# Four channel mixes of a MetaFormer block: fp32 matmuls on two row tiles in place of products of fp16 high and low halves

## The reference

```python
x = x + conv(_ln_c(x), w_pc, w_in, fft_w, w_out)      # _ln_c: normalised over the 48 channels
t = tokens(x); t = t + ffn(_ln_t(t), W1, b1, W2, b2)   # operands in fp8 e5m2, sums rounded to fp16

def conv(x, w_pc, w_in, fft_w, w_out):
    x1 = conv3x3(x[:, :12], w_pc)                      # 12 of the 48 channels
    x = concatenate([x1, x[:, 12:]], axis=1)
    x = conv1x1(x, w_in)                               # 48 -> 254 channels: the "mix"
    xf = rfft2(patches_8x8(x)) * fft_w                 # one weight for each channel and frequency
    a, b = split(irfft2(xf), 2, axis=1)
    return conv1x1(gelu(a, approximate=False) * b, w_out)   # 127 -> 48 channels
```

## Time and profile before

| | |
|---|---|
| median of 3 runs | 703.85 us (702.35 to 704.34) |
| the profiled execution's own time | 702.13 us |
| its span, first to last instruction | 700.3 us |
| mean granted clock of TensorE | 0.988 |
| matmuls (PE) busy | 664.4 us, 95% |
| weight loads (PEld) busy | 522.9 us, 75% |
| VectorE (DVE) busy | 596.9 us, 85% |
| ScalarE (ACT) busy | 536.6 us, 77% |
| GpSimd (POOL) busy | 460.9 us, 66% |

### The profile page before, as it was taken

How to read it: one execution, slowest core, us unless ns; L and a number is a source line. 1 busy time by engine, 2 the same in 40 slices (tenths; PEclk the granted TensorE clock), 3 DMA queues, 4 the chain that set the end, 5 groups by cost and what they waited for, 6 DMA issues and landing times.

```text
span 700.3 us, 19259 instructions
## 1 busy us (share of the span) xinstructions
PE 664.4 (95%) x6713; PEld 522.9 (75%) x6713; DVE 596.9 (85%) x1151; ACT 536.6 (77%) x1080; POOL 460.9 (66%) x355
## 2 busy tenths in 40 slices
PE   1689999999999999999999999999999999999984
PEld 1577778877777788777877887778778877787751
DVE  5537888889898889898999888988988899877877
ACT  3144479888888898888888988888889888877784
POOL 2555656778667767786776677867676777653353
PEclk9999999999999999999999999999999999999995
DMA  3443333333434343344344432343444324331102
GB/s 83 87 104 89 86 73 102 99 79 90 106 91 109 94 105 94 81 92 103 93 109 94 107 102 74 89 106 91 101 102 105 100 59 109 78 85 46 47 22 69
DMA packets 47959, 62.23 MB, mean 89 GB/s; under 512 B 20607, under 2 KB 36439, under 8 KB 47863
## 3 DMA queue, kind: packets, MB, share of 16 engines
q1 hardware_dynamic: 45015, 60.52, 34.9%
q10 hardware_dynamic: 2848, 0.48, 0.4%
HBM read 44.62 MB, written 16.35 MB: 87 GB/s over the span
## 4 chain that ended last, share of the span: by engine, by line
PE 87%; DVE 6%; SPq 2%; issue 2%; POOL 1%; ACT 1%; DMA 0%; DVEq 0%; ACTq 0%; POOLq 0%
PE inva L483 16%; PE invb L490 16%; PE mixp L470 13%; PE misc L734 8%; PE misc L499 7%; PE misc L554 4%; PE misc L520 4%; PE misc L598 4%; PE misc L470 3%; PE misc L719 3%; PE misc L529 2%; PE mixp L567 2%; PE misc L588 2%; PE mixp L574 2%; DVE gmix L1144 1%
## 5 line engine op out<-in xcount | busy, mean ns | idle before, releaser
L483 PEld LDWEIGHTS inva<-inv,gmix 128*127 128x127 f32 x1024 | 126.2, 191 | 16.5 <-DVE gmix L1144 11.5
L483 PE MATMUL inva<-inv,gmix 128*127 128x128 f32 x1024 | 137.9, 277 | 0.6 <-DVE gmix L1144 0.6
L490 PE MATMUL invb<-inv,gmix 128*127 128x128 f32 x1024 | 134.7, 274 | 0.2
L1144 DVE TENSOR_TENSOR gmix<-mixp,freq_w 128x508 f32<-128x508 f32 x192 | 122.7, 681 | 14.0 <-PE mixp L470 13.5
L1452 POOL TENSOR_TENSOR st<-st,neg_half 128x16 f32<-128x16 f32 x32 | 92.8, 2899 | 60.6 <-DVE st L1366 60.6
L490 PEld LDWEIGHTS invb<-inv,gmix 128*127 128x127 f32 x1024 | 123.7, 191 | 1.4 <-DVE hbuf L1155 0.6
L816 ACT ACTIVATE hid<-misc 128x512 f16<-128x512 f32 x180 | 98.0, 601 | 17.6 <-PE misc L554 17.6
L1155 DVE TENSOR_TENSOR hbuf<-gact,invb 127x512 f32<-127x512 f32 x128 | 87.5, 684 | 24.3 <-ACT gact L808 18.7
L1483 POOL TENSOR_TENSOR st<-st,neg_half 128x16 f32<-128x16 f32 x31 | 95.4, 3077 | 16.4 <-DVE st L1223 16.4
L825 ACT ACTIVATE hid<-hid 128x512 fp8e5<-128x512 f16 x174 | 93.2, 618 | 0.0
L808 ACT ACTIVATE gact<-inva 127x512 f32<-127x512 f32 x128 | 76.9, 601 | 20.6 <-PE inva L483 20.0
(11 more groups left out here) (178 smaller groups left out, 1369.2 us busy)
## 6 DMA issues: line engine op xcount, KB each, us to landing
xin<-in_x_dram SPq DMA_DIRECT2D x64, 192.0 KB, 3.3
xres<-in_x_dram SPq DMA_DIRECT2D x64, 192.0 KB, 4.2
out_dram<-ob SPq DMA_DIRECT2D x60, 192.0 KB, 2.7
taps<-cz_scratch SPq DMA_DIRECT2D x32, 292.5 KB
crm<-rm_scratch SPq DMA_DIRECT2D x64, 96.0 KB
cz_scratch<-cz SPq DMA_DIRECT2D x64, 48.8 KB
cx<-in_x_dram SPq DMA_DIRECT2D x32, 96.0 KB
rm_scratch<-rm_t SPq DMA_DIRECT2D x120, 4.0 KB
```

The source lines that it names most:

```text
L483: mm = pe.matmul(inva[0:HID, q * PX:(q + 1) * PX], gmix[:, s % 2, q, 0:HID], inv[:], start=True, stop=True, skip_group_check=True)
L490: mm = pe.matmul(invb[0:HID, q * PX:(q + 1) * PX], gmix[:, s % 2, q, HID:HID2], inv[:], start=True, stop=True, skip_group_check=True)
L1144: dve.tensor_tensor(gmix[:, s % 2, 2 * q:2 * q + 2, 0:HID2], pair[q][:, 0:2 * HID2].rearrange("p (e c) -> p e c", e=2), freq_w[:], ALU.mul ...
```

## The change

The coefficients are copied once, in fp32, to `zc` (by the same ScalarE instruction), and `win` is one fp32 matrix on both row tiles. A mix is then four fp32 matmuls in place of 16 fp16 ones. The subtraction `low_parts` and its semaphore go, and what waited for `lo_ready` waits for `coef_ready`, which ScalarE's copy raises. At the end of the kernel `zh` also served as a buffer for the last result; a tile `y_last` of its own takes that place.

```diff
-        win32 = sb("win32", [KC, HID2])
-        win = sb("win", [128, 2, HID2], F16)
+        win = sb("win", [128, HID2])
...
-        zh = sb("zh", [128, PAIRS, 128], F16)
-        zl = sb("zl", [128, PAIRS, 128], F16)
+        zc = sb("zc", [128, PAIRS, 128])
+        y_last = sb("y_last", [SPAN, PAIRS, PX], F16)
...
                 for e in range(2):
-                    for zpart, wpart in ((zh, 0), (zl, 0), (zh, 1), (zl, 1)):
-                        for q in range(2):
-                            r0 = HALF * q
-                            mm = pe.matmul(pair[q][:, e * HID2:(e + 1) * HID2],
-                                           zpart[r0:r0 + KC, 2 * s + e, :], win[r0:r0 + KC, wpart, :],
-                                           start=(e == 0 and zpart is zh and wpart == 0),
-                                           stop=(zpart is zl and wpart == 1), skip_group_check=True)
-                            if e == 1 and zpart is zl and wpart == 1:
-                                mm.then_inc(mix_done, 1)
+                    for q in range(2):
+                        y0 = HALF * q
+                        mm = pe.matmul(pair[q][:, e * HID2:(e + 1) * HID2], zc[y0:y0 + KC, 2 * s + e, :],
+                                       win[y0:y0 + KC, :], start=(e == 0), stop=True, skip_group_check=True)
+                        if e == 1:
+                            mm.then_inc(mix_done, 1)
...
-                        act.activation(zh[0:KSPAN, 4 * q:4 * q + 4, :].rearrange("p i c -> p (i c)"),
-                                       bank[(3, 0)[q]][0:KSPAN, :], ACT.Copy).then_inc(hi_ready, 1)
+                        act.activation(zc[0:KSPAN, 4 * q:4 * q + 4, :].rearrange("p i c -> p (i c)"),
+                                       bank[(3, 0)[q]][0:KSPAN, :], ACT.Copy).then_inc(coef_ready, 1)
...
-                dve.tensor_scalar(win32[:], inva[0:KC, 0:HID2], SCALE, None, ALU.mult).then_inc(set_dve, 1)
+                for base in (0, HALF):
+                    dve.tensor_scalar(win[base:base + KC, :], inva[0:KC, 0:HID2], SCALE, None, ALU.mult)\
+                       .then_inc(set_dve, 1)
...
-                for base in (0, HALF):
-                    dve.tensor_copy(win[base:base + KC, 0, :], win32[:]).then_inc(set_dve, 1)
...
-                dve.tensor_tensor(win[0:KC, 1, :], win32[:], win[0:KC, 0, :], ALU.subtract).then_inc(set_dve, 1)
...
-                dve.tensor_copy(win[HALF:HALF + KC, 1, :], win[0:KC, 1, :]).then_inc(set_done, 1)
-                dve.wait_ge(set_done, 1)
+                dve.sem_inc(set_done, 1)
...
-            def low_parts(t, q):
-
-                n = at(t, 3)
-                dve.wait_ge(hi_ready, upto(2 * n + q + 1))
-                dve.tensor_tensor(zl[0:KSPAN, 4 * q:4 * q + 4, :].rearrange("p i c -> p (i c)"),
-                                  bank[(3, 0)[q]][0:KSPAN, :],
-                                  zh[0:KSPAN, 4 * q:4 * q + 4, :].rearrange("p i c -> p (i c)"),
-                                  ALU.subtract).then_inc(lo_ready, 1)
...
-                if live(t, 3):
-                    low_parts(t, 0)
-                    low_parts(t, 1)
```

More of the change, by code:

```diff
@@ L193, in metaformer_kernel @@
         conv_read = sem("conv_read")
-        hi_ready = sem("hi_ready")
+        coef_ready = sem("coef_ready")
         gelu_ready = sem("gelu_ready")
@@ L212, in metaformer_kernel @@
         mr_ready = sem("mr_ready")
-        lo_ready = sem("lo_ready")
         gmix_ready = sem("gmix_ready")
@@ L460, in mix @@
                     if s % 2 == 0:
-                        pe.wait_ge(lo_ready, s // 2 + 1)
+                        pe.wait_ge(coef_ready, s // 2 + 1)
                 elif s == 0:
-                    pe.wait_ge(lo_ready, upto(2 * n + 2))
+                    pe.wait_ge(coef_ready, upto(2 * n + 2))
                 pe.wait_ge(gmix_ready, upto(8 * n + 2 * (s if s != 1 else 0)))
@@ L639, in drain @@
                 t = (0, DRAIN)
-                pe.wait_ge(lo_ready, 2 * STEPS)
+                pe.wait_ge(coef_ready, 2 * STEPS)
                 pe.wait_ge(h_ready, 4 * NEW + 2)
@@ L704, in step @@
                     pe.wait_ge(conv_read, upto(before(2)))
-                    pe.wait_ge(lo_ready, upto(2 * before(3)))
+                    pe.wait_ge(coef_ready, upto(2 * before(3)))
                     pe.wait_ge(tsq_ready, upto(2 * before(4)))
@@ L744, in step @@
                     mix(t, 0)
-                    pe.wait_ge(lo_ready, upto(2 * n + 2, 2 * STEPS))
+                    pe.wait_ge(coef_ready, upto(2 * n + 2, 2 * STEPS))
                     pe.wait_ge(xsq_ready, upto(2 * a + 2, 2 * STEPS))
@@ L748, in step @@
                 if live(t, 4):
-                    pe.wait_ge(lo_ready, upto(2 * n + 1, 2 * STEPS))
+                    pe.wait_ge(coef_ready, upto(2 * n + 1, 2 * STEPS))
                     project(t, 0, bank[3])
@@ L976, in drain @@
                 sum_half(OLD, 1, inva, y16)
-                sum_half(NEW, 0, bank[2], zh)
+                sum_half(NEW, 0, bank[2], y_last)
                 convert(NEW, 1, 0)
-                sum_half(NEW, 1, invb, zh)
+                sum_half(NEW, 1, invb, y_last)
                 for half in range(2):
@@ L1092, in setup @@
                     dve.tensor_copy(freq_w[:, e, :], mixp[1][:, 0:HID2]).then_inc(set_dve, 1)
-                dve.wait_ge(set_dve, 12 + 14)
+                dve.wait_ge(set_dve, 12 + 15)
                 dve.tensor_copy(l1h[:], l1[:]).then_inc(set_dve, 1)
@@ L1096, in setup @@
                 dve.tensor_copy(eye8[:], eye[:], saturate=False).then_inc(set_dve, 1)
-                for base in (0, HALF):
-                    dve.tensor_copy(win[base:base + KC, 0, :], win32[:]).then_inc(set_dve, 1)
                 dve.tensor_copy(wpc[:, :, 0:CC], pc32[:]).then_inc(set_dve, 1)
+                dve.wait_ge(set_dve, 12 + 18)
+                dve.tensor_tensor(wpc[:, :, CC:2 * CC], pc32[:], wpc[:, :, 0:CC], ALU.subtract).then_inc(set_dve, 1)
                 dve.wait_ge(set_dve, 12 + 19)
-                dve.tensor_tensor(win[0:KC, 1, :], win32[:], win[0:KC, 0, :], ALU.subtract).then_inc(set_dve, 1)
-                dve.tensor_tensor(wpc[:, :, CC:2 * CC], pc32[:], wpc[:, :, 0:CC], ALU.subtract).then_inc(set_dve, 1)
-                dve.wait_ge(set_dve, 12 + 21)
-                dve.tensor_copy(win[HALF:HALF + KC, 1, :], win[0:KC, 1, :]).then_inc(set_done, 1)
-                dve.wait_ge(set_done, 1)
+                dve.sem_inc(set_done, 1)
                 second_channels()
@@ L1108, in setup @@
                 dve.tensor_copy(b8[:], raw_b[:], saturate=False).then_inc(set_dve, 1)
-                dve.wait_ge(set_dve, 12 + 22)
+                dve.wait_ge(set_dve, 12 + 20)
                 dve.tensor_copy(bq[:], b8[:]).then_inc(set_dve, 1)
-                dve.wait_ge(set_dve, 12 + 23)
+                dve.wait_ge(set_dve, 12 + 21)
             def second_channels():
@@ L1296, in output_half @@
                                       tch[0:SPAN, NEW % 4, 4 * c:4 * c + 4].rearrange("p i (r w) -> p i r w", w=TW),
-                                      zh[0:SPAN, 4 * c:4 * c + 4, :].rearrange("p i (r w) -> p i r w", w=TW),
+                                      y_last[0:SPAN, 4 * c:4 * c + 4, :].rearrange("p i (r w) -> p i r w", w=TW),
                                       ALU.add).then_inc(late_out, 1)
@@ L1328, in drain @@
                 bias_half(OLD, 1, y16)
-                bias_half(NEW, 0, zh)
+                bias_half(NEW, 0, y_last)
                 output_half(0)
-                bias_half(NEW, 1, zh)
+                bias_half(NEW, 1, y_last)
                 output_half(1)
```

## The result

The changed kernel took 709.43 us (median of 5 runs, 707.83 to 709.82) where the kernel before, timed beside it, took 704.34: ratio 1.0076, 95% interval 1.0054 to 1.0098. It is 0.8% slower. Its profiled execution took 707.83 us, 5.70 more than that of before, over a span 5.7 longer.

A forecast was written before the change was run, and what follows sets the result against it. The prediction took TensorE's own instruction stream as the bound. Streaming -1.3, entries +8.9 and prologue -0.7 us summed to +6.9 on 703.85, so 710.7 us; its own range was 705.7 to 714, for 8 in 10 702 to 725.

The forecast's parts named there:

- The forecast case: Whole kernel: 710.7 us, 1.0% slower; 706 to 714 us given a chance of 0.68.
- the prologue term: VectorE's work before the steps: three kinds of operation go, one copy comes, taken as -0.7 us, or 0 if L1119's data is late.
- What bounds the kernel: Steady steps: only TensorE's own instruction stream sets the time; 0.1 us in a step's stream is 3.2 us over 32 steps.
- The freed VectorE time: VectorE without the subtractions: some 42 us less busy, worth nothing, turning into idle time ahead of gate L1155.
- Streaming: TensorE's matmuls inside a mix: 0.860 us in fp32 against 0.870 in fp16, -1.3 us over 128 mixes.
- The entry: First matmul after a tiling change, mixes 0, 2 and 3: 102 ns excess instead of 9, +8.9 us over 96 entries.
- The choice of L483's row over L499's: Entry excess taken from an fp32 row of 127 columns, 102 ns, not one of 64 columns, 50 ns, giving +3.9 us.
- The step: One pipeline step: 20.17 us in place of 19.96, +0.21, with TensorE still busy throughout.
- Entry free: Rival for the first matmul after a tiling change: fp32 load hides like fp16's, 701.9 us, not slower; chance 0.10.
- Loads one after the other: Rival for the mixes: two row tiles load in turn, entry 204 ns, +20.3 us in all, 724 us; chance 0.09.
- Strict order: Rival for the mixes: records start strictly in order, one distance more a run, +20.6 us on top, 731 us; chance 0.07.
- No overlap: Rival for the mixes: fp32 row tiles don't run side by side, +110 us on top, 820 us; chance 0.06.

The follow-up runs named there:

- Experiments 3: Kernel before the change without VectorE's two subtractions a step, mixes using the high half twice: 702.31 us, ratio 0.9999.
- experiment 5: Changed kernel with VectorE's two subtractions put back in their original form, read from the banks, mixes waiting for them, result unused: 707.98 us, ratio 1.008.
- Experiment 1: Changed kernel with mix 3 moved behind two of the three first-layer matmuls that followed it, one fp32 entry less: 707.1 us, ratio 1.0066.
- experiment 6: Changed kernel, mixes 0 and 1 in 64-column pieces: 707.99 us; in 32-column pieces with mix 3 moved behind two first-layer matmuls: 706.09 us.
- experiment 7: Changed kernel with a mix's loops exchanged, both patch pairs of row tile 0 before both of tile 1: 711.52 us, ratio 1.0132.
- experiment 8: Kernel before the change without the product of the two low halves: 690.3 us; two variants also weighing mix 0 earlier on VectorE: 703.84 and 699.83 us.
- last variant of experiment 8: Kernel before the change with three products, mix 0 weighed ahead of the three short operations that end the statistics: 699.83 us, ratio 0.9955.
- experiment 4: Changed kernel plus two dummy VectorE subtractions a step, both operands from SBUF, result unused: 719.72 us, ratio 1.0242.

## Why the prediction was right

The forecast case came about: 709.43 us against 710.7, by the mechanism named, with 5.7 us measured (by spans) against 6.9 summed. That the sum is so near is in part luck: the prologue term was 0.7 us off one way, single longer steps 0.9 and the steps at both ends 1.0 the other way.

**What bounds the kernel.** Right. Experiments 3 and 5 take the subtractions away and put them back without moving a step; the stream alone counts in the usual step. The freed VectorE time turned up as idle time ahead of the gate, as said. What the prediction didn't see is how near VectorE was: the second layer's first weight load starts 0.115 us behind the end of mix 0's weighing, its first matmul at the earliest 0.146 behind it, and in the usual step of before that matmul comes 0.218 behind it. So 0.07 us were to spare there, and 0.14 in the changed kernel, whose longer mix 0 stands behind the start of that chain.

**Streaming.** 0.857 us for a mix measured, 0.860 estimated, in pairs. The interpolation from 128 and 512 columns held to 1 ns a slot.

**The entry.** 104 ns measured for 102 taken, 96 times, on both tiles' loads under one excess. Experiment 1 removes one and gets 0.095 us back, experiment 6 shows that it goes with the columns of the load. The choice of L483's row over L499's, by the columns, was the one that mattered. The Trainium skill, "TensorE: Matmul & The Clock Gate", section on weight-path perf modes, has the fast weight load for 128 non-fp32 weights alone, and the runs agree in kind. From its column rule the prediction worked out an estimate of 80 ns for the difference; here it is 104 - 9 = 95. That estimate took a quarter of the load's time for the fast load, which the section's table gives as theory for fp8; for fp16 weights the trace has loads of 93 ns against 187 in fp32, a half.

**The step.** 20.17 predicted and measured (+0.21 summed, +0.22 measured). 28 full steps at +0.22 are 6.15 us. The prediction took the difference for all 32.

**The prologue term failed.** -0.7 was taken, -0.04 came: the first operation on the channels starts at 28.00 instead of 28.04, the first forward transform at 41.69 instead of 41.73. VectorE's last operation ahead of the channel work ended at 27.37, near the 27.3 foreseen, and then this row:

```profile
27.18 0.19 DVE L1096 TENSOR_TENSOR wpc<-pc,wpc 72x36 f16<-72x36 f32 x1
28.00 0.42 DVE L1112 TENSOR_TENSOR cz<-cx,crm 96x256 f32<-96x256 f32 x1 [0.63 <-DMA crm<-rm_scratch]
```

The case was named (data not there earlier makes it 0) and the wrong side chosen: the trace of before showed no wait there, because VectorE itself was late, and I took that for data that was ready.

**What offset it.** The three steps that fill the pipeline grew by 0.16, 0.16 and 0.15 us, 0.47 in all: their entries grew like the others', but 0.06 to 0.08 us in each came off a wait of TensorE for another engine. The last step's mixes stand in the tail, which took 45.96 us in both. Single steps longer than the rest made up 1.46 us in the execution of before and 0.58 in that of after, -0.89. So 6.15 + 0.47 - 0.04 - 0.89 = 5.69 of the 5.7. The prediction had no term for such steps, and took the 0.7 us of waits for all there was. By distances between starts it was 1.2 us in four steps: the list counts only from where the matmul before is modelled to have ended. In all four, and in the three of the changed kernel, the second layer's first matmul starts 0.146 us behind the end of the weighing, so VectorE was what was late. A fifth step of before is 0.17 us longer ahead of mix 0, where the trace names VectorE's subtraction once. Whether the change alters the number of such steps is not shown, since each kernel has one trace: without the subtractions experiment 1 had 1.8 us of them, with them experiment 5 had 0.7.

**The rivals.** *Entry free*: out, by the 478 ns. *Loads one after the other*: out, one excess of 104 ns for two tiles, and distances of 0.214. *Strict order*: out by the pairs, and by experiment 7, where even four records of one tile in a row don't hold back the other. The Trainium skill's sentence on the same page, that matmuls start strictly in program order, doesn't fit two tiles with records of different tiles queued like this; the measurement decides. *No overlap*: out.

## What to carry to other kernels

When TensorE's stream is full, count in distances between starts, and give each run of same-tiled matmuls an entry cost of its own: here 0.1 us more for an fp32 load of 128 columns, on top of a streaming cost that was level. Work removed from an engine that waits for TensorE brings nothing, and its measure is an experiment that puts it back in exactly the same form (operands in the same memory). On VectorE beside a busy GpSimd, moving an operation by one microsecond can cost more than the wait it was moved for: look at what each operation will then stand beside. And a list of waits that is nearly empty says little of the slack behind it: measure how long ahead of its use each result is ready (here 0.07 us).

## What the runs showed of the hardware that was not expected

**VectorE operations held by GpSimd.** In the kernel before this happens in every step where it costs nothing: L1217, 16 elements, takes 0.80 us and ends 0.03 behind GpSimd's L1479, and L1204, 1024 elements in fp16, takes 1.44 where it takes 0.48 in the last variant of experiment 8. Rarely it costs something: L1359, 16 elements, usually 0.17 us, takes 0.63, and ends 0.02 to 0.03 us behind GpSimd's L1420. VectorE, GpSimd, the weighing and the weight load behind it, and what TensorE's second layer then waits:

```profile
201.52 0.63 DVE L1359 SCALAR_TENSOR_TENSOR st<-st 128x16 f32<-128x16 f32 x1
...
201.47 0.66 POOL L1420 TENSOR_TENSOR cz<-cz 96x256 f16<-96x256 f32 x1
...
203.08 0.68 DVE L1144 TENSOR_TENSOR gmix<-mixp,freq_w 128x508 f32<-128x508 f32 x1
203.88 0.17 PEld L567 LDWEIGHTS mixp<-hid,l 128*64 128x64 fp8e5 x4 [1.08 <-issue]
203.91 0.62 PE L567 MATMUL mixp<-hid,l 128*64 128x512 fp8e5 x4 [0.23 <-DVE gmix L1144]
```

The weighing ends at 203.76, the load starts 0.12 behind it. Such meetings stand ahead of all four longer steps of before at the second layer (in one of them at L1349 alone), and ahead of one of the changed kernel's three; in the other two the gate or the weighing itself started some 0.35 us late, and what held it the trace doesn't say. The variants of experiment 8 made the same thing happen at L1211 in every step, for 1.6 us, and experiment 4 shows both sides slower. That a short operation waits for the end of the other is shown by the ends, 0.03 to 0.04 us apart; that it is the memory port they share was not tested. The Trainium skill, "SBUF — State Buffer", section "SBUF: two separate sides", has this as a lock held for the whole instruction, also against VectorE operations with two SBUF operands; the runs agree, and by it the dummy of experiment 4, with both operands in SBUF, had to be expected to meet GpSimd's addition.

**The load sizes.** fp32 loads take 187, 133 and 106 ns at 128, 64 and 32 columns, 0.83 ns a column over a fixed 80, the same slope as the excess.

**Left open.** Why the gap of some 0.09 us at each change of the tiling is the same for fp16 and fp32, and what held the gate and the weighing in those two longer steps of the changed kernel, was not tried.
